# A state-space layer: scan results and their products with C share one ring of four chunks, and GpSimd multiplies in place

## The chip, the cores and the metric

The kernel runs on one core of one Trainium2 chip. A core has five engines that run their own instruction streams and meet at semaphores: TensorE (PE in the profile, its weight loads PEld), VectorE (DVE), ScalarE (ACT), GpSimd (POOL) and SyncE (SP), which here issues DMAs. The metric is the device time of one execution in microseconds (us), lower is better.

## The reference, cut to what matters

The whole program is a tower of nine layers on 8 images of 257 tokens. The change lies in one layer, a bidirectional state-space layer with 512 inner channels and 32 states for each:

```python
def step(h, ins):
    dt_t, B_t, C_t, u_t = ins
    dA = jnp.exp(dt_t[..., None] * A)
    h = dA * h + (dt_t * u_t)[..., None] * B_t[:, None, :]
    y = jnp.einsum('bdn,bn->bd', h, C_t)
    return (h, y)
_, ys = jax.lax.scan(step, h0, xs)          # 257 tokens
y = ys.transpose(1, 0, 2) + uc * Dp
y = y * _silu(z)
```

It runs forward over each image with one set of weights and backward with another.

## The kernel before, in words

The layer is `section_mamba`. It treats 16 units one after the other: 8 images forward, then 8 backward. Channels lie on the 128 partitions in four blocks j. A unit has 16 chunks n: q = n // 4 is a group of 8 states, j = n % 4 a block of channels. A chunk is a tile of 128 x 8 x 256 numbers (8 states, the first 256 tokens), and is cut into four parts m of two states each.

For a part, the engines work as a line:

- ScalarE writes the decays exp(dt * A) into `da` (two chunks deep, line 2326).
- TensorE spreads B over the partitions into PSUM `pb` (four parts deep, `spread_b`, line 2114). In chunks 4 to 15 the last part comes ready multiplied from transposes instead (`turn_products`, line 2101).
- VectorE multiplies `pb` by dt * u (`product`, line 2494; not for the turned parts), then scans the part into `hs` (line 2513).
- GpSimd multiplies half a chunk of `hs` (four states) by C, which lies in `cb`, into `hc` (line 2013), two halves to a chunk. Between them it copies the states of token 255 into `h_l` (line 2012).
- TensorE adds up the eight states of a chunk with matmuls against the identity into PSUM `py` (`total`, line 2127).

`hs` and `hc` hold two chunks each. The order of every engine's stream is written out by hand. TensorE's step (n, m) is: spread part 4n + m + 2, then `total` of part m of chunk n - 2, then other work. So `total` of the first half of a chunk stands ahead of the spreads that VectorE needs two chunks later. VectorE, before it scans part p, makes the product for part p + 1; that stands ahead of the scan in its stream. Before the first scan of chunk n it waits until GpSimd has multiplied all of chunk n - 2 (`hc_done`). GpSimd starts the first half of chunk n when two of its parts are scanned (`b_free`) and when TensorE has added up chunk n - 2 (`y_free`); it starts the second half when all four are scanned.

Between chunks the engines do the rest of the unit and prepare the next one. On GpSimd: after chunk 0 `last_token` (the 257th token of the unit before, by five small instructions, lines 1979 to 1986) and three memsets; in chunk 2 `last_gate` (lines 1992 and 1995); after chunks 3 and 4 `taps` (three adds each, line 1935, the convolution of the next unit); small `cut`s after 8 and 9; after 10 line 1974; after 11 `cut_low` (lines 1949 and 1950); after 12 and 13 `soften` (lines 1958 to 1960). On TensorE: `outward` (line 2138) at the four steps of chunk 5, projections for the next unit (line 2058) at the steps (6,1), (6,2), (7,0) and (7,1), `b_c_rank` at (8,0). On ScalarE: `take_z` follows the projections of chunks 6 and 7 and ends with a Silu and a table load; only then come the decays of chunk 8 and the scaled transposes `tp` (line 2348). VectorE reduces the last token's sum (`out_last`, line 2471) after the first scan of chunk 2; for this it waits for `last_token`.

Of the kernel before, what the change touches and what calls it, by code (L numbers as in the profile page):

```python
# [1781 lines left out]
def section_mamba(nc, k, con, dirs, bfuse, normed=0):  # L1782
# [6 lines left out]
    L = T - 1  # L1789
    open_section(nc, k, "mamba")  # L1790
    with ExitStack() as ctx:
# [21 lines left out]
        hs = sb("hs", [P, 2, NQ_, L])  # L1813
        hc = sb("hc", [P, 2, NQ_, L])
# [11 lines left out]
                 "sqd var std scaled normed f_done f_out conv_link soft_link soft_low soft_top last_link act_head act_tail").split()  # L1826
# [48 lines left out]
        with nc.Block() as block:  # L1875
# [43 lines left out]
            def _(pool):  # L1919
# [77 lines left out]
                def body(u, v, d, before, after):  # L1997
                    scanned, summed = Turn(u, SUB, 4), Turn(u, NCH, 2)
                    for n in range(NCH):
                        q, j = n // DJ, n % DJ  # L2000
                        if j == 0:
                            pool.wait_ge(s["c_odd" if q % 2 else "c_even"], Turn(u, 32)(16 * (q // 2 + 1)))
                        for half in range(2):
                            part_ = slice(4 * half, 4 * half + 4)
                            pool.wait_ge(s["b_free"], scanned(4 * n + 2 * half + 2))
                            if half == 0:
                                pool.wait_ge(s["y_free"], summed(n - 1))
                            settle(pool, k)
                            if (n, half) == (2, 1) and before is not None:
                                last_gate(u - 1, 1 - v)  # L2010
                            if half:
                                nc.gpsimd.tensor_copy(h_l[:, v, j, q * NQ_:(q + 1) * NQ_], hs[:, n % 2, :, L - 1])
                            nc.gpsimd.tensor_tensor(hc[:, n % 2, part_], hs[:, n % 2, part_], cb[:, q % 2, part_, :], ALU.mult).then_inc(s["hc_done"], 1)  # L2013
                        if n == 0 and before is not None:
                            last_token(u - 1, 1 - v, before)
                        if n == 10:
                            last_rate(u, v, d)
                        if after is not None:
                            if n == 0:
                                pool.wait_ge(s["dt_set"], Turn(u, DJ)(DJ))  # L2020
                                settle(pool, k)
                                lead(1 - v)
                            if n in (3, 4):
                                taps(u + 1, 1 - v, n - 3)
                            if n in (8, 9):
                                cut(u + 1, n - 8)
                            if n == 11:
                                cut_low(u + 1, 1 - v, 0, 4, 0)
                            if n == 12:
                                soften(u + 1, 1 - v, 0, 2, 4)  # L2030
                            if n == 13:
                                soften(u + 1, 1 - v, 2, 4, 8)
# [16 lines left out]
            def _(pe):  # L2049
# [67 lines left out]
                def total(u, v, d, n, m):  # L2117
# [7 lines left out]
                    for o in range(2):  # L2125
                        st = 2 * m + o
                        ins = nc.tensor.matmul(sums(j), k.ident[:], hc[:, n % 2, st, :], start=False, stop=(q == QN - 1 and st == NQ_ - 1 and j % 2 == 1))  # L2127
# [311 lines left out]
            def _(dve):  # L2439
# [56 lines left out]
                def body(u, v, d, before, after):  # L2496
                    for n in range(NCH):
                        for m in range(4):
# [6 lines left out]
                            if m == 0:  # L2505
                                dve.wait_ge(s["hc_done"], Turn(u, 2 * NCH, 16)(2 * n - 2))
# [6 lines left out]
                            nc.vector.tensor_tensor_scan(two(hs[:, n % 2, 2 * m:2 * m + 2, :]), two(da[:, n % 2, 2 * m:2 * m + 2, :]), two(pb[:, p % 4]), 0.0, ALU.mult, ALU.add).then_inc(s["b_free"], 1)  # L2513
# [1059 lines left out]
```

## Time and profile before

| what | us |
|---|---|
| median of 3 runs | 3731.81 (3726.15 to 3732.51) |
| the profiled execution | 3738.08 |
| its span | 3736.3 |
| first to last start of the scans of line 2513 | 1168.9 to 2972.6 |
| busy in the whole span | PE 3177.2, DVE 2509.6, ACT 2060.3, POOL 1907.3 |

The page gives, for each engine, busy time; the span in 40 slices; then the groups of instructions with the idle time of the engine in front of them and what ended it. The layer takes some 1,800 of the 3,736 us. In its slices VectorE stands at nine tenths or more, TensorE at eight, GpSimd at eight or nine, ScalarE at seven. A timeline row gives a start, a length, an engine and a line; in square brackets stand the idle time ahead of it and who ended it. "x2" is two instructions without a gap.

### The profile page before, as it was taken

Reading aid. Unit: us, or ns where it says so; the run is one execution under the profiler, and the core shown is the slowest. Engines: PE = TensorE matmul, PEld = TensorE weight load, DVE = VectorE, ACT = ScalarE, POOL = GpSimd, SP = SyncE. Lnnn points to the kernel's source line nnn. Section 1 sums busy time; section 2 is a strip of 40 time slices with the busy share of each in tenths; the row PEclk is TensorE's granted clock in tenths of the full one; section 3 lists DMA queues with packets and bytes.
Section 4 is the critical chain, followed back from the end, with each engine's and each line's share of the span. In section 5 each row is a group of like instructions: output and inputs, shape, how many; then the busy total and the mean of one; then the engine's idle time right before and its main releaser. Section 6 shows DMA issues by size and latency. Waiting matters only on the chain. (4 is left out here: it accounts for less than half of the span.)

```text
span 3736.3 us, 61028 instructions
## 1 busy us (share of the span) xinstructions
PE 3177.2 (85%) x19916; PEld 2391.4 (64%) x19916; DVE 2509.6 (67%) x3780; ACT 2060.3 (55%) x4490; POOL 1907.3 (51%) x1672
## 2 busy tenths in 40 slices
PE   0959989989986889888888888898888887999957
PEld 0649976668974566666666666666665665666544
DVE  6351126653126999999999999999999833666541
ACT  0232225551226778777777778777777433666522
POOL 0013312200315898898888898988898600000024
PEclk9779989999997999999999999999999997999965
DMA  3039930012951111111111111111111000000036
GB/s 104 1 122 332 334 112 2 2 42 104 331 200 64 35 36 46 36 35 47 35 49 46 35 37 35 47 35 35 36 46 35 23 12 15 2 2 2 1 96 200
DMA packets 134796, 262.22 MB, mean 70 GB/s; under 512 B 13792, under 2 KB 106328, under 8 KB 123960
## 3 DMA queue, kind: packets, MB, share of 16 engines
q1 hardware_dynamic: 124568, 230.99, 18.8%
q0 software_dynamic: 9888, 27.01, 2.2%
q8 instruction: 175, 2.87, 0.3%
q14 instruction: 165, 1.35, 0.1%
HBM read 233.42 MB, written 24.55 MB: 69 GB/s over the span
## 5 line engine op out<-in xcount | busy, mean ns | idle before, releaser
L2013 POOL TENSOR_TENSOR ssm_hc<-ssm_hs,ssm_cb 128x1024 f32<-128x1024 f32 x512 | 1205.3, 2358 | 178.0 <-PE ssm_py L2127 157.9
L2513 DVE TENSOR_TENSOR_SCAN ssm_hs<-ssm_da,ssm_pb 128x512 f32<-128x512 f32 x1024 | 1222.0, 1208 | 96.0 <-POOL ssm_hc L2013 91.3
L2127 PE MATMUL ssm_py<-ssm_hc,ident 128*128 128x256 f32 x4096 | 1069.2, 384 | 39.2 <-POOL ssm_hc L2013 39.2
L2326 ACT ACTIVATE ssm_da<-ssm_dt,ssm_an 128x255 f32<-128x255 f32 x2048 | 863.8, 498 | 194.1 <-DVE ssm_hs L2513 155.5
L2127 PEld LDWEIGHTS ssm_py<-ssm_hc,ident 128*128 128x128 f32 x4096 | 709.8, 192 | 119.4 <-POOL ssm_hc L2013 47.2
L2494 DVE TENSOR_TENSOR ssm_pb<-ssm_pb,ssm_dtu 128x512 f32<-128x512 f32 x832 | 563.7, 678 | 49.1 <-PE ssm_pb L2114 25.6
L2114 PE MATMUL ssm_pb<-ssm_bst,ssm_eyeb 96*128 96x256 bf16 x1664 | 327.9, 279 | 140.3 <-DVE ssm_hs L2513 121.8
L2114 PEld LDWEIGHTS ssm_pb<-ssm_bst,ssm_eyeb 96*128 96x128 bf16 x1664 | 133.1, 99 | 346.2 <-DVE ssm_hs L2513 248.7
L3353 DVE TENSOR_TENSOR moe_hid<-moe_pu,moe_actg 128x512 f32<-128x512 f32 x71 | 49.1, 692 | 349.1 <-PE moe_pu L2988 349.1
L2988 PEld LDWEIGHTS moe_pu<-moe_xt,moe_up 128*128 128x128 f32 x2272 | 266.8, 193 | 6.4 <-ACT moe_xt L3113 3.0
L2988 PE MATMUL moe_pu<-moe_xt,moe_up 128*128 128x128 f32 x2272 | 267.8, 277 | 1.8 <-ACT moe_xt L3113 1.8
L2858 POOL DMA_INDIRECT moe_xr<-moe_x_dram,moe_rowx x71 | 69.0, 971 | 334.1 <-PE ln_ps L2975 180.0
L1662 DVE TENSOR_REDUCE duo_mxr<-duo_pairs 128x4 f32<-128x1024 f32 x128 | 156.7, 1224 | 101.8 <-PE duo_pairs L1400 76.7
L1570 ACT ACTIVATE duo_ex<-duo_pairs 128x1024 f32<-128x1024 f32 x128 | 131.0, 1023 | 98.0 <-PE duo_pairs L1400 97.9
L2101 PE MATMUL ssm_pb<-ident,ssm_tp 128*128 128x128 f32 x768 | 119.7, 279 | 47.7 <-ACT ssm_tp L2348 34.4
L1396 PE MATMUL duo_pairs<-duo_k,duo_q 32*128 32x256 f32 x1024 | 151.5, 413 | 9.0 <-DVE duo_mxr L1662 3.7
L1400 PE MATMUL duo_pairs<-duo_q,duo_k 32*128 32x256 f32 x1024 | 145.0, 399 | 1.2 <-ACT duo_ex L1570 1.1
L2101 PEld LDWEIGHTS ssm_pb<-ident,ssm_tp 128*128 128x128 f32 x768 | 92.4, 142 | 80.1 <-DVE ssm_hs L2513 52.4
L2058 PE MATMUL ln_ps<-x,ssm_win 128*128 (+1 forms) x512 | 134.7, 387 | 4.0 <-DVE x L351 1.8
L3003 PE MATMUL ln_ps<-moe_down,moe_hid 128*128 128x256 f32 x568 | 134.5, 380 | 1.1 <-ACT moe_yo L3134 1.1
L2864 POOL DMA_INDIRECT moe_y_dram<-moe_yo,moe_rowy x71 | 70.2, 988 | 118.9 <-ACT moe_yo L3134 118.9
L2348 ACT ACTIVATE ssm_tp<-ssm_dtut,ssm_bt 128x512 f32<-128x512 f32 x192 | 125.2, 708 | 0.0
(591 smaller groups left out, 5195.8 us busy)
## 6 DMA issues: line engine op xcount, KB each, us to landing
moe_up<-in_moe_up SPq DMA_DIRECT2D x72, 1024.0 KB, 6.1
ssm_cb<-ssm_c_dram SPq DMA_DIRECT2D x64, 1024.0 KB, 5.6
moe_down<-in_moe_down SPq DMA_DIRECT2D x72, 512.0 KB, 7.1
sw_wt<-in_sw_w SPq DMA_DIRECT2D x64, 192.5 KB
moe_x_dram<-moe_tok SPq DMA_DIRECT2D x32, 128.0 KB
moe_yg<-moe_y_dram SPq DMA_DIRECT2D x16, 256.0 KB, 3.3
tok_w<-in_wd SPq DMA_DIRECT2D x4, 576.0 KB, 12.8
out<-h SPq DMA_DIRECT2D x1, 2056.0 KB, 6.4
```

Source lines behind the costliest of these rows:

```text
L1396: ins1 = nc.tensor.matmul(dst1[:, o, at], q[r, b1, t * P:t * P + P], kk[r, b1, a, 0:256], start=True, stop=True)
L1400: ins2 = nc.tensor.matmul(dst2[:, o, at], kk[r, b2, a, t * P:t * P + P], q[r, b2, 0:256], start=True, stop=True)
L1662: released(nc.vector.tensor_reduce(mxr[:, u % 2, a, 2 * jp:2 * jp + 2, :], bank("s1", u, a, jp).rearrange("p o (t s) -> p o t s", t=2), AX ...
L2013: nc.gpsimd.tensor_tensor(hc[:, n % 2, part_], hs[:, n % 2, part_], cb[:, q % 2, part_, :], ALU.mult).then_inc(s["hc_done"], 1)
L2058: ins = nc.tensor.matmul(pm[:, n % 2, 0:T], w_in[:, c, n * P:n * P + P], row, start=(c == 0), stop=(c == C - 1))
L2101: ins = nc.tensor.transpose(pb[:, p % 4, o, h * P:h * P + P], tp[:, TURNED.index(q) % 2, o, h, j * P:j * P + P], k.ident[:])
L2114: ins = nc.tensor.matmul(pb[:, p % 4, o, :], one_state(st), bst2[:, v, 0:L], start=True, stop=True)
L2127: ins = nc.tensor.matmul(sums(j), k.ident[:], hc[:, n % 2, st, :], start=False, stop=(q == QN - 1 and st == NQ_ - 1 and j % 2 == 1))
L2326: ins = nc.scalar.activation(da[:, n % 2, 2 * m + o, 1:L], dt2[:, v, j, 1:L], ACT.Exp, scale=a_n[:, d, j, st:st + 1])
L2494: nc.vector.tensor_tensor(b2, b2, dtu2[:, v, j:j + 1, 0:L].broadcast_to([P, 2, L]), ALU.mult).then_inc(s["b_set"], 1)
L2513: nc.vector.tensor_tensor_scan(two(hs[:, n % 2, 2 * m:2 * m + 2, :]), two(da[:, n % 2, 2 * m:2 * m + 2, :]), two(pb[:, p % 4]), 0.0, ALU.m ...
L2988: ins = nc.tensor.matmul(pu[:, b % 2, g, j * P:j * P + P], up[:, b % WR, c, g * HID + j * P:g * HID + j * P + P], xt[:, b % 2, c, :], star ...
```

## The change

`hs` becomes a ring of four chunks and `hc` goes away. GpSimd multiplies each half of a chunk in place in `hs`. Since that destroys the states, the copy of token 255's states now comes before both halves, after all four parts are scanned, and GpSimd waits for its own copy (a new semaphore `h_kept`) before it multiplies. Its wait for `y_free` goes. `last_gate` moves from the middle of chunk 2 to the front of chunk 3. TensorE's `total` reads `hs`. VectorE's wait before chunk n is now for `y_free` of chunk n - 4, in place of `hc_done` of chunk n - 2.

```diff
+    RING = 4
-        hs = sb("hs", [P, 2, NQ_, L])
-        hc = sb("hc", [P, 2, NQ_, L])
+        hs = sb("hs", [P, RING, NQ_, L])
...
                 def body(u, v, d, before, after):
-                    scanned, summed = Turn(u, SUB, 4), Turn(u, NCH, 2)
+                    scanned = Turn(u, SUB, 4)
                     for n in range(NCH):
                         q, j = n // DJ, n % DJ
                         if j == 0:
                             pool.wait_ge(s["c_odd" if q % 2 else "c_even"], Turn(u, 32)(16 * (q // 2 + 1)))
+                        pool.wait_ge(s["b_free"], scanned(4 * n + 4))
+                        if n == 3 and before is not None:
+                            last_gate(u - 1, 1 - v)
+                        settle(pool, k)
+                        nc.gpsimd.tensor_copy(h_l[:, v, j, q * NQ_:(q + 1) * NQ_], hs[:, n % RING, :, L - 1]).then_inc(s["h_kept"], 1)
+                        pool.wait_ge(s["h_kept"], Turn(u, NCH)(n + 1))
                         for half in range(2):
-                            part_ = slice(4 * half, 4 * half + 4)
-                            pool.wait_ge(s["b_free"], scanned(4 * n + 2 * half + 2))
-                            if half == 0:
-                                pool.wait_ge(s["y_free"], summed(n - 1))
-                            settle(pool, k)
-                            if (n, half) == (2, 1) and before is not None:
-                                last_gate(u - 1, 1 - v)
-                            if half:
-                                nc.gpsimd.tensor_copy(h_l[:, v, j, q * NQ_:(q + 1) * NQ_], hs[:, n % 2, :, L - 1])
-                            nc.gpsimd.tensor_tensor(hc[:, n % 2, part_], hs[:, n % 2, part_], cb[:, q % 2, part_, :], ALU.mult).then_inc(s["hc_done"], 1)
+                            part_ = hs[:, n % RING, 4 * half:4 * half + 4, :]
+                            nc.gpsimd.tensor_tensor(part_, part_, cb[:, q % 2, 4 * half:4 * half + 4, :], ALU.mult).then_inc(s["hc_done"], 1)
...
                     for o in range(2):
                         st = 2 * m + o
-                        ins = nc.tensor.matmul(sums(j), k.ident[:], hc[:, n % 2, st, :], start=False, stop=(q == QN - 1 and st == NQ_ - 1 and j % 2 == 1))
+                        ins = nc.tensor.matmul(sums(j), k.ident[:], hs[:, n % RING, st, :], start=False, stop=(q == QN - 1 and st == NQ_ - 1 and j % 2 == 1))
...
-                            if m == 0:
-                                dve.wait_ge(s["hc_done"], Turn(u, 2 * NCH, 16)(2 * n - 2))
+                            if m == 0 and (n >= RING or before is not None):
+                                dve.wait_ge(s["y_free"], Turn(u, NCH, 2)(n - RING + 1))
                             dve.wait_ge(s["da_done"], Turn(u, SUB)(p + 1))
...
-                            nc.vector.tensor_tensor_scan(two(hs[:, n % 2, 2 * m:2 * m + 2, :]), two(da[:, n % 2, 2 * m:2 * m + 2, :]), two(pb[:, p % 4]), 0.0, ALU.mult, ALU.add).then_inc(s["b_free"], 1)
+                            nc.vector.tensor_tensor_scan(two(hs[:, n % RING, 2 * m:2 * m + 2, :]), two(da[:, n % 2, 2 * m:2 * m + 2, :]), two(pb[:, p % 4]), 0.0, ALU.mult, ALU.add).then_inc(s["b_free"], 1)
```

Two lines fewer stand above line 2013, so that later lines move up by two; the multiply is line 2011 and the copy line 2007 afterwards.

On GpSimd, in a unit that has one before it, chunk 1 to the front of chunk 3 stood like this (the rows L2013 are halves of chunks 1, 1, 2, 2 and 3):

```order
337 L2013 TENSOR_TENSOR ssm_hc<-ssm_hs,ssm_cb 128x1024
338 L2005 REGISTER_ALU
339 L2012 COPY ssm_hl<-ssm_hs 128x8
340 L2013 TENSOR_TENSOR ssm_hc<-ssm_hs,ssm_cb 128x1024
341 L2005 REGISTER_ALU
342 L2007 REGISTER_ALU
343 L2013 TENSOR_TENSOR ssm_hc<-ssm_hs,ssm_cb 128x1024
344 L2005 REGISTER_ALU
345 L1992 TENSOR_TENSOR ssm_yl<-ssm_yl 128x4
346 L1993 REGISTER_ALU
347 L1995 TENSOR_TENSOR ssm_zs<-ssm_zs,ssm_yl 128x4
348 L2012 COPY ssm_hl<-ssm_hs 128x8
```

Now the same place holds chunk 2, `last_gate`, and chunk 3 with the `taps` behind it:

```order
327 L2003 REGISTER_ALU
328 L2007 COPY ssm_hl<-ssm_hs 128x8
329 L2008 REGISTER_ALU
330 L2011 TENSOR_TENSOR ssm_hs<-ssm_hs,ssm_cb 128x1024 x2
331 L2003 REGISTER_ALU
332 L1992 TENSOR_TENSOR ssm_yl<-ssm_yl 128x4
333 L1993 REGISTER_ALU
334 L1995 TENSOR_TENSOR ssm_zs<-ssm_zs,ssm_yl 128x4
335 L2007 COPY ssm_hl<-ssm_hs 128x8
336 L2008 REGISTER_ALU
337 L2011 TENSOR_TENSOR ssm_hs<-ssm_hs,ssm_cb 128x1024 x2
338 L1932 ISA
```

The copy has moved from between the halves to ahead of them, and the gate from inside chunk 2 to ahead of chunk 3's copy.

At the head of such a unit, chunk 0 and `last_token` stood like this:

```order
319 L2013 TENSOR_TENSOR ssm_hc<-ssm_hs,ssm_cb 128x1024
320 L2005 REGISTER_ALU
321 L2012 COPY ssm_hl<-ssm_hs 128x8
322 L2013 TENSOR_TENSOR ssm_hc<-ssm_hs,ssm_cb 128x1024
323 L1979 TENSOR_TENSOR ssm_yl<-ssm_uc,ssm_cols 128x4
324 L1981 TENSOR_TENSOR ssm_tl<-ssm_dtu,ssm_bcl 128x128
```

Now:

```order
308 L2007 COPY ssm_hl<-ssm_hs 128x8
309 L2008 ISA
310 L2011 TENSOR_TENSOR ssm_hs<-ssm_hs,ssm_cb 128x1024 x2
311 L1979 TENSOR_TENSOR ssm_yl<-ssm_uc,ssm_cols 128x4
```

Both halves now stand behind the copy, ahead of `last_token`.

## Rows read from the trace of the kernel before

**Rows 1.** Page, groups: count, busy and mean ns, idle before and releaser.
```profile
L2013 POOL TENSOR_TENSOR ssm_hc<-ssm_hs,ssm_cb 128x1024 f32<-128x1024 f32 x512 | 1205.3, 2358 | 178.0 <-PE ssm_py L2127 157.9
L2513 DVE TENSOR_TENSOR_SCAN ssm_hs<-ssm_da,ssm_pb 128x512 f32<-128x512 f32 x1024 | 1222.0, 1208 | 96.0 <-POOL ssm_hc L2013 91.3
```

**Rows 2.** Waits of DVE in the layer, 1169 to 2973: total us, times, longest.
```profile
DVE ssm_hs L2513 <- POOL ssm_hc L2013: 91.3, 46, 2.7
DVE ssm_pb L2494 <- PE ssm_pb L2114: 25.6, 22, 2.6
```

**Rows 3.** Windows of two units: length, busy PE, PEld, DVE, ACT, POOL; PEclk.
```profile
1620.97:1736.01 115.04, 98.56 (x502) 74.34 (x501) 106.06 (x124) 85.54 (x193) 100.71 (x76) 0.99 0.13 39
1736.01:1849.00 112.99, 98.07 (x509) 74.01 (x507) 105.64 (x124) 85.47 (x193) 100.54 (x76) 1.00 0.13 39
```

**Rows 4.** Timeline of DVE, one unit and the next's head.
```profile
2309.00 1.21 DVE L2513 TENSOR_TENSOR_SCAN ssm_hs<-ssm_da,ssm_pb 128x512 f32<-128x512 f32 x1
...
2330.35 1.21 DVE L2513 TENSOR_TENSOR_SCAN ssm_hs<-ssm_da,ssm_pb 128x512 f32<-128x512 f32 x1
...
2352.75 1.22 DVE L2513 TENSOR_TENSOR_SCAN ssm_hs<-ssm_da,ssm_pb 128x512 f32<-128x512 f32 x1 [1.76 <-POOL ssm_hc L2013]
...
2364.34 0.70 DVE L2494 TENSOR_TENSOR ssm_pb<-ssm_pb,ssm_dtu 128x512 f32<-128x512 f32 x1 [1.29 <-PE ssm_pb L2114]
...
2384.26 1.21 DVE L2513 TENSOR_TENSOR_SCAN ssm_hs<-ssm_da,ssm_pb 128x512 f32<-128x512 f32 x1
...
2407.33 1.22 DVE L2513 TENSOR_TENSOR_SCAN ssm_hs<-ssm_da,ssm_pb 128x512 f32<-128x512 f32 x1 [1.89 <-POOL ssm_hc L2013]
...
2416.24 1.22 DVE L2513 TENSOR_TENSOR_SCAN ssm_hs<-ssm_da,ssm_pb 128x512 f32<-128x512 f32 x1 [2.57 <-POOL ssm_hc L2013]
...
2431.71 0.26 DVE L2471 TENSOR_REDUCE ssm_yl<-ssm_tl 128x4 f32<-128x128 f32 x1
```

**Rows 5.** Timeline of POOL, the same unit.
```profile
2310.37 0.19 POOL L2012 COPY ssm_hl<-ssm_hs 128x8 f32<-128x8 f32 x1 [0.24 <-DVE ssm_hs L2513]
...
2314.15 0.46 POOL L1985 TENSOR_TENSOR ssm_tl<-ssm_tl,ssm_hl 128x128 f32<-128x128 f32 x1
2314.68 0.46 POOL L1986 TENSOR_TENSOR ssm_tl<-ssm_tl,ssm_bcl 128x128 f32<-128x128 f32 x1
...
2325.00 0.20 POOL L1992 TENSOR_TENSOR ssm_yl<-ssm_yl 128x4 f32<-128x4 f32 x1 [0.50 <-DVE ssm_hs L2513]
...
2325.52 0.19 POOL L2012 COPY ssm_hl<-ssm_hs 128x8 f32<-128x8 f32 x1
2325.68 2.36 POOL L2013 TENSOR_TENSOR ssm_hc<-ssm_hs,ssm_cb 128x1024 f32<-128x1024 f32 x1
...
2332.10 2.36 POOL L2013 TENSOR_TENSOR ssm_hc<-ssm_hs,ssm_cb 128x1024 f32<-128x1024 f32 x1
...
2347.83 2.35 POOL L2013 TENSOR_TENSOR ssm_hc<-ssm_hs,ssm_cb 128x1024 f32<-128x1024 f32 x1 [0.33 <-POOL ssm_e L1935]
...
2386.22 0.19 POOL L2012 COPY ssm_hl<-ssm_hs 128x8 f32<-128x8 f32 x1
...
2413.53 0.19 POOL L2012 COPY ssm_hl<-ssm_hs 128x8 f32<-128x8 f32 x1
...
2418.28 0.19 POOL L2012 COPY ssm_hl<-ssm_hs 128x8 f32<-128x8 f32 x1
```

**Rows 6.** Timeline of PE, the same unit.
```profile
2351.18 1.03 PE L2127 MATMUL ssm_py<-ssm_hc,ident 128*128 128x256 f32 x4
...
2362.57 0.65 PE L2101 MATMUL ssm_pb<-ident,ssm_tp 128*128 128x128 f32 x4 [2.33 <-ACT ssm_tp L2348]
...
2404.81 1.88 PE L2127 MATMUL ssm_py<-ssm_hc,ident 128*128 128x256 f32 x4 [1.22 <-POOL ssm_hc L2013]
```

**Rows 7.** Timeline of the layer's end, all engines.
```profile
2970.31 3.43 DVE L2513 TENSOR_TENSOR_SCAN ssm_hs<-ssm_da,ssm_pb 128x512 f32<-128x512 f32 x3
...
2974.18 2.36 POOL L2013 TENSOR_TENSOR ssm_hc<-ssm_hs,ssm_cb 128x1024 f32<-128x1024 f32 x1
```

More of the change, by code:

```diff
@@ L1825, in section_mamba @@
                  "dt_free dt_exp dt_set crow_in c_out c_even c_odd dtut_done dtut_in tp_in b_done b_free da_done b_set hc_done y_free ys_done o_done o_out "
-                 "sqd var std scaled normed f_done f_out conv_link soft_link soft_low soft_top last_link act_head act_tail").split()
+                 "sqd var std scaled normed f_done f_out conv_link soft_link soft_low soft_top last_link act_head act_tail h_kept").split()
         s = {n: signal(nc, k.sems, "ssm_" + n) for n in names}
```

## The prediction

> **What bounds the kernel now.** I read the groups of the page first. Only the state-space layer is touched, and its two longest groups are GpSimd's multiply and VectorE's scan, which wait for each other: the scan has 91.3 us of idle time in front of it that GpSimd ended, the multiply 157.9 us that TensorE's sums ended [rows 1]. The waits of VectorE inside the layer come next: 91.3 us in 46 pieces of at most 2.7 us for GpSimd, 25.6 us for TensorE's spreads [rows 2]. Then the windows of whole units: in a unit of 112.99 us VectorE is busy 105.64, GpSimd 100.54 and TensorE 98.07 [rows 3]. So VectorE sets the pace with 7.3 us of idle time in a unit, GpSimd has only 5 us less work, and TensorE 7.6 us less. Taking a buffer's limit away can give at most those idle microseconds, and two engines stand close behind.
>
> Last I walked through one unit, to see where the waits are. There are three for GpSimd: 1.76 us at chunk 7, 1.89 at chunk 15 and 2.57 at chunk 0 of the next unit; and one of 1.29 us for a spread, at the product for chunk 9's first part, right behind the first [rows 4]. They come where GpSimd's other work is thick: the taps after chunks 3 and 4, and `cut_low` and `soften` after 11 to 13.
>
> **The change part by part.** I write S(n) for the start of the fourth scan of chunk n, and count from it.
>
> Removed, VectorE's wait for chunk n - 2. It is not the last link between GpSimd and VectorE: TensorE's stream still holds the `total` of chunk n - 2 ahead of the spreads that VectorE needs for the last part of chunk n and for chunk n + 1, and that `total` still waits for GpSimd. So VectorE's freedom grows by about half a chunk, not by two. The new wait, for the sum of chunk n - 4, lies behind that one always, and I cost it at nothing.
>
> Removed, GpSimd's wait for `y_free` (the 157.9 us). It costs nothing now where GpSimd would have waited for scans anyway, and the next item replaces it by a later release.
>
> Moved, the copy ahead of both halves. GpSimd now starts a chunk when its fourth part is scanned, not the second. The copy that waits for the fourth scan today starts 1.37 us after that scan's start (2309.00 to 2310.37) [rows 4, 5]. So copy(n) is at S(n) + 1.37 at the earliest.
>
> Added, the wait for its own copy. The trace has linked small instructions: 2314.15 to 2314.68 is 0.53 us for a length of 0.46, so 0.07 more than the length; copy to multiply without link is 0.16 us (2325.52 to 2325.68) [rows 5]. 0.19 + 0.07 - 0.16 = 0.10 us in each chunk. Bounds: nothing, if it hides, and 0.2 if the register instruction ahead of the wait counts too. 256 times 0.1 would be 26 us of GpSimd's work, of which only what lies on a path counts, below. The multiply itself, in place, keeps its 2.36 us.
>
> Moved, `last_gate`: 0.52 us (2325.00 to 2325.52) [rows 5], now in front of chunk 3, behind the wait for its fourth scan and ahead of the taps. TensorE needs it only in chunk 5, behind a `total` that waits longer.
>
> *The tight place at the unit's seam.* From S(11), at 2384.26, the reduction of `out_last` starts after 47.45 us (2431.71) [rows 4], 4.46 of it the waits at chunks 15 and 0; VectorE's own work is 43.0. Afterwards GpSimd's path is: copy(11) at 1.37; copy 11 to copy 14 takes 27.31 now [rows 5], with three links 27.6; chunks 14 and 15 take 4.75 each (2413.53 to 2418.28), with links 9.7; from copy(0) to the end of `last_token` 4.77 now (2310.37 to 2314.68 + 0.46), and then 2.36 more, since the copy stands ahead of both halves, and 0.1: 7.2. With 0.1 to reach VectorE the sum is 46.0 us. VectorE is there at 43.0, so it waits 3 us, part of it for the spreads behind `total` of chunk 14, the rest at the reduction, which waits for nothing today. Today's way takes 47.45. Gain 1.5 us a unit. The new late one is `out_last`.
>
> *The tight place at chunks 3 to 8.* TensorE's `total` of chunk 5's first half starts at 2351.18, that is S(3) + 20.83, 1.00 us after that half is multiplied (2347.83 + 2.35) [rows 4 to 6]. Afterwards: copy(3) at 1.37 + 0.52 = 1.89; the second half of chunk 3 at 1.89 + 0.26 + 2.36 = 4.51; from there to chunk 5 is 15.73 us now (2332.10 to 2347.83), 15.83 with the link; copy(5) at 20.34, its first half done at 20.34 + 0.26 + 2.35 = 22.95. So TensorE must wait 2.1 us longer before this `total`. Behind it stand the last two projections, behind them ScalarE's `take_z`, and behind that the decays of chunk 8 and the `tp` for which TensorE waits 2.33 us at 2362.57 [rows 6]. That chain, not GpSimd, is what VectorE meets at chunks 8 and 9: it waits 1.29 us there although it has just lost 1.76 [rows 4]. Without the 1.76 it would wait 3.05; after the change 3.05 + 2.1. Loss 2.1 us a unit. The wait for GpSimd that disappears at chunk 7 pays nothing.
>
> *The end.* The last scans end at 2973.74 and the last multiply at 2976.54, 2.80 later [rows 7]. Afterwards 1.37 - 1.21 for the copy's start, 0.26 to the first half, and 2 x 2.36: 5.1. Loss 2.3 us, once.
>
> Each seam comes 15 times and so do the taps. Sum: 15 x 2.1 - 15 x 1.5 + 2.3 = 11.3 us. Against the profiled execution's own 3738.08 that gives 3749.4; it stood 6.3 above the median of the runs, so against the median 3731.8 it gives 3743.
>
> **The rivals.**
>
> *A. TensorE's chain stretches.* If the `total` of chunk 5 is not what holds the projections, or ScalarE makes up for it, only the seam counts: 3731.8 - 22.5 + 2.3 = 3712. For it: TensorE is busy for 98 of a unit's 113 us [rows 3], so it has some air. Against it: between chunk 5 and chunk 8 the timeline shows it without a gap.
>
> *B. The ring does all it can:* every wait for GpSimd goes and none comes: 3731.8 - 91.3 + 2.3 = 3643. Against it: the spread wait behind chunk 7, and GpSimd's path at the seam, which is work and not waiting.
>
> *C. The two places cancel.* 0.5 us off either estimate moves the sum by 7.5 us; 3732.
>
> *D. TensorE's clock.* TensorE waits longer in two places of each unit. Where it has waited 1.22 us for GpSimd, four matmuls take 1.88 us in place of 1.03 [rows 6], the lower of its two levels; a unit in which such a fall meets the spreads takes 115.04 us in place of 112.99 [rows 3]. I count three such units in the trace. If the longer waits make it so in the other twelve: 12 x 2.05 = 24.6 more, 3768. It decides from the point where the longer gaps at chunks 7 and 0 bring a fall in most units.
>
> The Trainium skill, in "TensorE: Matmul & The Clock Gate", Part 1, says that the clock is gated by how busy the engine has been, half rate when idle; by that rule longer waits speak for this rival, and the trace agrees in its one case above but shows no general rate.
>
> **How the numbers follow.** My sum has 0.42, A 0.20, B 0.06, C 0.17, D 0.15. What a measurement here can tell from no change is about 0.2%, 7.5 us. Faster by more: A and B, 0.26. Slower by more: D and nearly all of my case, 0.53. Within: C and the rest, 0.21. The likeliest case's own range is 3735 to 3755 (0.5 us in each place, 0.1 in each link). Leaving out B and the far end of D, 3708 to 3770.
>
> **What would show it.** Right: the waits of the scan for GpSimd nearly gone from the waits of VectorE, but idle time for spreads and decays at chunks 8 and 9 of 4 to 5 us a unit; the reduction of line 2469 waiting for GpSimd, 0.5 to 3 us in 15 units; TensorE waiting some 2 us for GpSimd ahead of the `total` in chunk 7; units of 113.5 to 114 us. Wrong: no such wait of TensorE there and units under 112.5 (A), under 108 (B); units of 115 and more with PEclk below 0.97 (D); a multiply that isn't 2.36 us in place.

## The result, and the profile after

| | before | after |
|---|---|---|
| median of 6 runs, side by side | 3732.16 us (3720.88 to 3732.90) | 3751.77 us (3741.60 to 3766.17) |
| the profiled execution | 3738.08 us | 3746.07 us |

The ratio is 1.0063, with a 95% interval of 1.0036 to 1.0090: the changed kernel is slower, by 19.6 us between the medians. The forecast was 11.3 us more, 3743.

The groups of the page that answer to [rows 1]:

```profile
L2511 DVE TENSOR_TENSOR_SCAN ssm_hs<-ssm_da,ssm_pb 128x512 f32<-128x512 f32 x1024 | 1219.6, 1205 | 20.7 <-ACT ssm_da L2324 17.7
L2125 PE MATMUL ssm_py<-ssm_hs,ident 128*128 128x256 f32 x4096 | 1105.5, 394 | 119.6 <-POOL ssm_hs L2011 119.4
L2011 POOL TENSOR_TENSOR ssm_hs<-ssm_hs,ssm_cb 128x1024 f32<-128x1024 f32 x512 | 1195.1, 2355 | 20.9 <-POOL ssm_hl L2007 0.4
L2492 DVE TENSOR_TENSOR ssm_pb<-ssm_pb,ssm_dtu 128x512 f32<-128x512 f32 x832 | 564.3, 678 | 152.0 <-PE ssm_pb L2112 123.3
L2007 POOL COPY ssm_hl<-ssm_hs 128x8 f32<-128x8 f32 x256 | 49.2, 192 | 169.1 <-DVE ssm_hs L2511 147.2
```

The scan no longer waits for GpSimd, and GpSimd no longer waits for TensorE's sums. Both waits came back in other names. The sums wait 119.4 us for the products, GpSimd's copy 147.2 us for the scans, and VectorE's product 123.3 us for the spreads. The multiply in place takes what it took before, 2355 ns.

The waits inside the layer (total us, times, longest), which answer to [rows 2]:

```profile
DVE ssm_pb L2492 <- PE ssm_pb L2112: 123.3, 76, 4.4
PE ssm_py L2125 <- POOL ssm_hs L2011: 117.7, 59, 3.4
DVE ssm_hs L2511 <- ACT ssm_da L2324: 13.3, 12, 1.1
DVE ssm_yl L2469 <- POOL ssm_tl L1986: 2.4, 6, 0.5
```

VectorE's waits for GpSimd and for spreads were 91.3 + 25.6 = 116.9 us. Now the waits for spreads, decays and the last token are 139.0. So the change swapped one wait for a slightly larger one.

The windows of 14 units, from one reduction of the last token to the 14th after it, before and then after (columns as in [rows 3]):

```profile
1297.09:2885.33 1588.24, 1380.05 (x7050) 1043.05 (x7049) 1479.51 (x1737) 1195.56 (x2701) 1408.67 (x1048) 0.99 0.13 39
```

```profile
1294.53:2913.16 1618.63, 1412.46 (x7053) 1084.26 (x7052) 1483.39 (x1736) 1191.19 (x2703) 1415.28 (x1051) 0.96 0.13 39
```

A unit takes 113.45 us before and 115.62 after, so 2.17 us more; the forecast was 0.6. VectorE's and GpSimd's work is all but the same. PEclk fell from 0.99 to 0.96, and TensorE's busy time rose by 32 us.

To find where the 2.17 us lie, I took the starts of the fourth scans, S(n), in 13 whole units of each trace and averaged the stretches:

| stretch | before | after | forecast |
|---|---|---|---|
| S(3) to S(9) | 41.03 | 44.39 | +2.1 |
| S(9) to S(11) | 13.08 | 13.09 | 0 |
| S(11) to S(2) of the next unit | 52.55 | 51.44 | -1.5 |
| S(2) to S(3) | 6.84 | 6.83 | 0 |

All of the loss is in the first row, and it has levels. In five of the 14 units after, S(3) to S(9) took 43.0 us, in three 43.5 to 44.2, and in six 45.2 to 45.7. Before, the undisturbed units took 40.8.

VectorE in an undisturbed unit of the kernel after, where S(3) is 2350.02 and S(9) is 2392.99:

```profile
2350.02 1.21 DVE L2511 TENSOR_TENSOR_SCAN ssm_hs<-ssm_da,ssm_pb 128x512 f32<-128x512 f32 x1
...
2377.30 0.70 DVE L2492 TENSOR_TENSOR ssm_pb<-ssm_pb,ssm_dtu 128x512 f32<-128x512 f32 x1 [2.70 <-PE ssm_pb L2112]
...
2380.81 1.22 DVE L2511 TENSOR_TENSOR_SCAN ssm_hs<-ssm_da,ssm_pb 128x512 f32<-128x512 f32 x1 [1.11 <-ACT ssm_da L2324]
...
2386.14 0.70 DVE L2492 TENSOR_TENSOR ssm_pb<-ssm_pb,ssm_dtu 128x512 f32<-128x512 f32 x1 [1.29 <-PE ssm_pb L2112]
...
2392.99 1.21 DVE L2511 TENSOR_TENSOR_SCAN ssm_hs<-ssm_da,ssm_pb 128x512 f32<-128x512 f32 x1
```

GpSimd in the same unit, up to the first half of chunk 5:

```profile
2351.43 0.20 POOL L1992 TENSOR_TENSOR ssm_yl<-ssm_yl 128x4 f32<-128x4 f32 x1 [1.93 <-DVE ssm_hs L2511]
...
2351.95 0.19 POOL L2007 COPY ssm_hl<-ssm_hs 128x8 f32<-128x8 f32 x1
2352.22 2.36 POOL L2011 TENSOR_TENSOR ssm_hs<-ssm_hs,ssm_cb 128x1024 f32<-128x1024 f32 x1
...
2370.48 4.65 POOL L2011 TENSOR_TENSOR ssm_hs<-ssm_hs,ssm_cb 128x1024 f32<-128x1024 f32 x2
```

TensorE in the same unit, at the `total` of chunk 5 and the projections behind it:

```profile
2372.87 1.13 PE L2125 MATMUL ssm_py<-ssm_hs,ident 128*128 128x256 f32 x4 [1.86 <-POOL ssm_hs L2011]
2373.84 1.03 PE L2056 MATMUL ln_ps<-x,ssm_win 128*128 x4
2374.70 0.60 PE L2099 MATMUL ssm_pb<-ident,ssm_tp 128*128 128x128 f32 x4
2375.14 1.03 PE L2125 MATMUL ssm_py<-ssm_hs,ident 128*128 128x256 f32 x4
2376.01 1.03 PE L2056 MATMUL ln_ps<-x,ssm_win 128*128 x4
2376.87 0.39 PE L2112 MATMUL ssm_pb<-ssm_bst,ssm_eyeb 96*128 96x256 bf16 x2
```

This `total` starts at S(3) + 22.85, two us later than in [rows 6], and the spread for which VectorE waits 2.70 us is the last row. Behind the second projection stands ScalarE's `take_z`, then the decays of chunk 8 (line 2324) and the transposes `tp` (line 2346), for which TensorE waits:

```profile
2377.07 0.38 ACT L2255 ACTIVATE ssm_zs<-ln_ps 128x257 f32<-128x257 f32 x1 [1.78 <-PE ln_ps L2056]
...
2379.72 3.29 ACT L2324 ACTIVATE ssm_da<-ssm_dt,ssm_an 128x255 f32<-128x255 f32 x8
2382.92 1.32 ACT L2346 ACTIVATE ssm_tp<-ssm_dtut,ssm_bt 128x512 f32<-128x512 f32 x2
2384.37 0.65 PE L2099 MATMUL ssm_pb<-ident,ssm_tp 128*128 128x128 f32 x4 [2.33 <-ACT ssm_tp L2346]
```

VectorE's second and third wait, 1.11 and 1.29 us, are for these decays and for the spread behind these transposes. Its three waits sum to 5.1 us.

The same place in a disturbed unit (S(3) = 1885.21), first TensorE, then VectorE:

```profile
1908.07 1.98 PE L2125 MATMUL ssm_py<-ssm_hs,ident 128*128 128x256 f32 x4 [1.87 <-POOL ssm_hs L2011]
1909.84 1.91 PE L2056 MATMUL ln_ps<-x,ssm_win 128*128 x4
```

```profile
1914.17 0.70 DVE L2492 TENSOR_TENSOR ssm_pb<-ssm_pb,ssm_dtu 128x512 f32<-128x512 f32 x1 [4.39 <-PE ssm_pb L2112]
```

The wait for GpSimd is the same, 1.87 us, but behind it TensorE runs at the lower of its two levels: 1.98 and 1.91 us in place of 1.13 and 1.03. VectorE's wait grows from 2.70 to 4.39. The windows S(3) + 21 to S(3) + 38 of these two units, the disturbed one first:

```profile
1906.21:1923.21 17.00, 12.81 (x54) 9.83 (x55) 10.02 (x11) 9.61 (x20) 13.76 (x8) 0.86 0.01 1
2371.02:2388.02 17.00, 12.82 (x68) 10.20 (x69) 11.90 (x14) 11.30 (x24) 13.72 (x8) 1.00 0.01 1
```

In that window PEclk was 1.00 in the five units of 43.0 us and below it in the other nine; before it was below 1.00 in 3 of 14.

At the seam behind the undisturbed unit, VectorE (at "issue" the trace names no releaser):

```profile
2432.13 1.21 DVE L2511 TENSOR_TENSOR_SCAN ssm_hs<-ssm_da,ssm_pb 128x512 f32<-128x512 f32 x1
2434.69 0.70 DVE L2492 TENSOR_TENSOR ssm_pb<-ssm_pb,ssm_dtu 128x512 f32<-128x512 f32 x1 [1.35 <-issue]
...
2440.32 0.70 DVE L2492 TENSOR_TENSOR ssm_pb<-ssm_pb,ssm_dtu 128x512 f32<-128x512 f32 x1 [1.79 <-PE ssm_pb L2112]
...
2443.30 0.70 DVE L2492 TENSOR_TENSOR ssm_pb<-ssm_pb,ssm_dtu 128x512 f32<-128x512 f32 x1 [0.86 <-PE ssm_pb L2112]
...
2453.58 0.26 DVE L2469 TENSOR_REDUCE ssm_yl<-ssm_tl 128x4 f32<-128x128 f32 x1
```

S(11) is 2406.06 here, so the reduction of this seam, one of the longest, comes after 47.52 us and waits for nothing. GpSimd's last token was ready 1.1 us before it:

```profile
2452.02 0.46 POOL L1986 TENSOR_TENSOR ssm_tl<-ssm_tl,ssm_bcl 128x128 f32<-128x128 f32 x1
```

Over 14 units GpSimd ended the last token 46.08 us after S(11), and the reduction came after 46.54 us on average (before: 47.67).

The end of the layer answers to [rows 7]:

```profile
2999.29 2.30 DVE L2511 TENSOR_TENSOR_SCAN ssm_hs<-ssm_da,ssm_pb 128x512 f32<-128x512 f32 x2
3001.76 0.19 POOL L2007 COPY ssm_hl<-ssm_hs 128x8 f32<-128x8 f32 x1 [0.71 <-DVE ssm_hs L2511]
3002.04 4.65 POOL L2011 TENSOR_TENSOR ssm_hs<-ssm_hs,ssm_cb 128x1024 f32<-128x1024 f32 x2
```

From the end of the scans to that of the multiplies it is 5.1 us, as forecast (2.80 before).

In this one pair of traces the 14 units are 30.4 us longer and the layer, from its first scan to its last, 32.9; the executions differ by only 8.0. The other 25 us lie outside the layer: up to its first scan the trace after is 5.1 us shorter (1163.8 in place of 1168.9), behind its last scan 19.9 (742.7 in place of 762.6). The 762.6 is the odd one: in the 11 other traces of this document that part takes 741 to 749 us. The interval of the ratio is 13 to 34 us and holds what the layer lost.

### The profile page after: what moved, and what is told of

Its sections match the earlier page's. It is cut to its first block and busy times, and to the rows that moved or that the text cites. A ratio compares the mean times of both kernels' runs of the same rounds, so it can differ in the third digit from the quotient of the medians.

```text
span 3744.3 us, 60553 instructions
## 1 busy us (share of the span) xinstructions
PE 3198.8 (85%) x19916; PEld 2426.2 (65%) x19916; DVE 2512.2 (67%) x3780; ACT 2054.2 (55%) x4490; POOL 1913.3 (51%) x1672
## 5 line engine op out<-in xcount | busy, mean ns | idle before, releaser
L2125 PE MATMUL ssm_py<-ssm_hs,ident 128*128 128x256 f32 x4096 | 1105.5, 394 | 119.6 <-POOL ssm_hs L2011 119.4
L2011 POOL TENSOR_TENSOR ssm_hs<-ssm_hs,ssm_cb 128x1024 f32<-128x1024 f32 x512 | 1195.1, 2355 | 20.9 <-POOL ssm_hl L2007 0.4
L2125 PEld LDWEIGHTS ssm_py<-ssm_hs,ident 128*128 128x128 f32 x4096 | 729.7, 197 | 215.4 <-POOL ssm_hs L2011 137.9
L2492 DVE TENSOR_TENSOR ssm_pb<-ssm_pb,ssm_dtu 128x512 f32<-128x512 f32 x832 | 564.3, 678 | 152.0 <-PE ssm_pb L2112 123.3
L2112 PEld LDWEIGHTS ssm_pb<-ssm_bst,ssm_eyeb 96*128 96x128 bf16 x1664 | 146.5, 100 | 237.5 <-DVE ssm_hs L2511 129.3
L2007 POOL COPY ssm_hl<-ssm_hs 128x8 f32<-128x8 f32 x256 | 49.2, 192 | 169.1 <-DVE ssm_hs L2511 147.2
```

Of the source, the lines that this page charges most:

```text
L2011: nc.gpsimd.tensor_tensor(part_, part_, cb[:, q % 2, 4 * half:4 * half + 4, :], ALU.mult).then_inc(s["hc_done"], 1)
L2112: ins = nc.tensor.matmul(pb[:, p % 4, o, :], one_state(st), bst2[:, v, 0:L], start=True, stop=True)
L2125: ins = nc.tensor.matmul(sums(j), k.ident[:], hs[:, n % RING, st, :], start=False, stop=(q == QN - 1 and st == NQ_ - 1 and j % 2 == 1))
L2492: nc.vector.tensor_tensor(b2, b2, dtu2[:, v, j:j + 1, 0:L].broadcast_to([P, 2, L]), ALU.mult).then_inc(s["b_set"], 1)
```

## The experiments

Each ran in five rounds beside the kernel before. The chips of the three groups gave 3720.25, 3708.95 and 3722.23 us for the kernel before, so the ratios count. The table has the stretches of the trace as above (13 units), the unit and PEclk over 14 units. These are of one traced execution each, the ratio is of all; the traced execution stood within 9 us of its kernel's median, but for "early in 3, 4, 5" (15 us under it), "filled at chunk 7" (15 above) and "later sums" (19 above). In the last three kernels VectorE's output products or its reduction stand in later chunks, so that 0.7 to 0.9 us of a unit have moved from the second stretch into the one from S(2) to S(3).

| kernel | S(3) to S(9) | S(11) to S(2) | unit | PEclk | ratio to before |
|---|---|---|---|---|---|
| before | 41.03 | 52.55 | 113.45 | 0.99 | 1 |
| after | 44.39 | 51.44 | 115.62 | 0.96 | 1.0063 [1.0036, 1.0090] |
| late start alone | 42.39 | 54.02 | 116.31 | 0.97 | 1.0132 [1.0093, 1.0170] |
| early start everywhere | 42.12 | 50.41 | 112.47 | 0.96 | 0.9959 [0.9931, 0.9986] |
| early in 3, 4, 5 | 41.61 | 51.34 | 112.86 | 0.97 | 1.0017 [0.9996, 1.0038] |
| early in 12 to 15, 0 | 44.64 | 52.51 | 117.02 | 0.95 | 1.0155 [1.0133, 1.0176] |
| early in 3 and 11 | 42.13 | 50.06 | 112.16 | 0.96 | 0.9922 [0.9891, 0.9953] |
| filled at the seam | 44.09 | 51.83 | 115.86 | 0.99 | 1.0090 [1.0061, 1.0120] |
| filled at chunk 7 | 43.46 | 51.36 | 114.78 | 0.96 | 1.0041 [1.0016, 1.0066] |
| later sums | 41.83 | 50.28 | 112.75 | 0.97 | 0.9951 [0.9926, 0.9976] |
| later sums, reduction later | 41.61 | 47.28 | 109.59 | 0.99 | 0.9877 [0.9851, 0.9903] |
| the same, early start everywhere | 41.37 | 47.26 | 109.36 | 0.99 | 0.9861 [0.9837, 0.9886] |

**The late start alone**, in the kernel before:

```diff
-                            pool.wait_ge(s["b_free"], scanned(4 * n + 2 * half + 2))
                             if half == 0:
+                                pool.wait_ge(s["b_free"], scanned(4 * n + 4))
                                 pool.wait_ge(s["y_free"], summed(n - 1))
...
-                            if half:
+                            if half == 0:
                                 nc.gpsimd.tensor_copy(
```

> The kernel before with one edit: GpSimd copies ahead of both halves and so starts a chunk after its fourth scan; scan results and products stay in separate buffers of two chunks, without the wait of GpSimd for its own copy. Theory L (the late start is what costs, the ring gives nothing because TensorE's order holds VectorE anyway): as slow as the changed kernel, 3744 to 3760, TensorE's waits for the products near 118 us in the layer, as after. Rival M (the ring gave something back, and the late start costs more than the difference shows): clearly slower than the changed kernel, 3765 or more, with VectorE's scans waiting over 91 us for GpSimd. Rival N (the cost lies in the multiply in place or in the link to the copy): not slower than before, 3725 to 3738.

Rival M holds: 1.0132, and the scans' wait for GpSimd grows from 91.3 to 148.5 us:

```profile
DVE ssm_hs L2513 <- POOL ssm_hc L2013: 148.5, 75, 2.7
PE ssm_py L2127 <- POOL ssm_hc L2013: 75.6, 56, 2.1
```

So the ring was not worth nothing. It gives back 2.6 us at the seam (54.02 to 51.44). Between chunks 3 and 9 it gives nothing back. There the late start alone costs 1.36 us a unit. By the forecast's own terms it should cost 2.1 less the gate (0.52) and three links (0.3), 1.3. The kernel after differs from this one in the links, the gate and GpSimd's missing wait for `y_free` too; no run tests these one by one.

**The early start given back everywhere**, with the ring kept:

```diff
-                        pool.wait_ge(s["b_free"], scanned(4 * n + 4))
                         if n == 3 and before is not None:
                             last_gate(u - 1, 1 - v)
-                        settle(pool, k)
-                        nc.gpsimd.tensor_copy(h_l[:, v, j, q * NQ_:(q + 1) * NQ_], hs[:, n % RING, :, L - 1]).then_inc(s["h_kept"], 1)
-                        pool.wait_ge(s["h_kept"], Turn(u, NCH)(n + 1))
                         for half in range(2):
+                            pool.wait_ge(s["b_free"], scanned(4 * n + 2 * half + 2))
+                            settle(pool, k)
+                            kept = slice(q * NQ_ + 4 * half, q * NQ_ + 4 * half + 4)
+                            nc.gpsimd.tensor_copy(h_l[:, v, j, kept], hs[:, n % RING, 4 * half:4 * half + 4, L - 1]).then_inc(s["h_kept"], 1)
+                            pool.wait_ge(s["h_kept"], Turn(u, 2 * NCH)(2 * n + half + 1))
```

> The changed kernel with the early start given back: GpSimd waits for two scans, copies four states, waits for that copy and multiplies that half in place; then the same for the other half; the gate of the last token stands ahead of chunk 3's waits. The ring of four stays. Theory L (late start): 3720 to 3738, TensorE's waits for the products fall from 118 us to under 60, units near 113. Its price is one more copy with its link in each chunk, 0.3 us of GpSimd. Rival N (in place or the links cost): stays at 3745 or more. Rival R (the ring gives something once the start is early): under 3720.

0.9959 in place of 1.0063, and faster than before. The late start is the cause: this kernel still multiplies in place and has twice as many copies with links, so these are not what made the other slower. The gate has come forward with the start, and no run moves it alone. Times the 3732 us before, 0.9959 is 3717, so that rival R holds beside theory L: with the early start the ring gives something. TensorE's wait for the products fell only to 69.5 us, not below 60. The group of the small copies shows their price, 46.8 us more of GpSimd's time than the 49.2 us of the whole copies:

```profile
L2009 POOL COPY ssm_hl<-ssm_hs 128x4 f32<-128x4 f32 x512 | 96.0, 188 | 80.1 <-DVE ssm_hs L2512 68.5
```

**Where the late start costs.** The same edit for some chunks alone, `if n in EARLY`. First chunks 3, 4 and 5:

> The changed kernel with the early start (four states copied after two scans, then multiplied, then the other half) in chunks 3, 4 and 5 alone, and the gate of the last token ahead of chunk 3's waits. Theory P (the loss lies where the prediction put it, in the chain from chunk 3 over the sum of chunk 5 and the projections to the decays of chunk 8, 2.1 us a unit): units of 113.2 to 114.0 us in place of 115.6, ratio to the kernel before 0.994 to 1.001. Rival S (it lies at the unit's seam, chunks 12 to 0): units stay at 115 or more, ratio 1.004 or more.

Theory P: S(3) to S(9) falls from 44.39 to 41.61, the seam stays, and the unit is 112.86, a little below the expected 113.2. The ratio, 1.0017, is a little above its 1.001, but its interval reaches to 0.9996 and, on the other side, just touches that of the changed kernel, so that what was gained rests on the trace. Then chunks 12 to 15 and 0:

> The changed kernel with the early start in chunks 12 to 15 and 0 alone. Theory P (the seam is no loss against the kernel before, since it takes 47.5 us from the fourth scan of chunk 11 in both): units of 114.6 to 115.6, what is gained comes only from a seam that gets shorter than before; ratio 1.001 to 1.007. Rival S (the late start costs at the seam): units of 113.9 or less, ratio under 1.000.

Neither: it is slower, 117.02. The last token now ends 47.46 us after S(11) in place of 46.08. Those 1.4 us are the five more copies at 0.28 us from copy to multiply (2351.95 to 2352.22 above). The reduction now waits for it in 12 units:

```profile
DVE ssm_yl L2475 <- POOL ssm_tl L1986: 11.2, 12, 1.3
```

Behind the start of chunk 11 GpSimd has no idle time worth the name at the seam, so starting its chunks earlier gives nothing and each added copy is paid in full. Ahead of chunk 11 it stands idle, in the changed kernel:

```profile
2407.44 0.19 POOL L2007 COPY ssm_hl<-ssm_hs 128x8 f32<-128x8 f32 x1 [1.52 <-DVE ssm_hs L2511]
```

That suggested the next one, chunks 3 and 11 alone, where its unbroken stretches begin:

> The changed kernel with the early start in two chunks alone, 3 and 11, and the gate ahead of chunk 3's waits. Theory H (GpSimd has work without a pause from chunk 3, with the taps, and from chunk 11, with the cut and the softening; only where such a stretch begins does the late start cost, behind it GpSimd is late anyway): the stretch S(3) to S(9) falls from 44.4 us to 41.0 to 42.2, S(11) to S(2) of the next unit from 51.4 to 49.0 to 50.2, units 110.5 to 112.3, ratio 0.980 to 0.993. Rival (every chunk's late start costs its part, as in the kernel with the early start in 12 to 15 and 0, which lost): S(11) to S(2) stays at 51 or more, units 113 or more.

Theory H: all four numbers in their ranges, if near their slow ends. The early start of chunk 11 takes 1.4 us off the seam, where five early chunks inside it added 1.1. GpSimd ends the last token 44.74 us after S(11) in place of 46.08, so 1.3 us earlier, for the 1.52 for which it had stood idle.

**TensorE's clock.** Matmuls of no use in TensorE's waits; first at the seam:

```diff
+                            if after is not None and (n, m) in ((14, 2), (15, 0), (15, 2)):
+                                for _ in range(6):
+                                    nc.tensor.matmul(pm[:, 1, 0:L], k.ident[:], uc2[:, v, 0, 0:L], start=True, stop=True)
```

> The changed kernel with six matmuls of no use (into the free half of the bank of sums for projections) ahead of TensorE's waits in the steps (14,2), (15,0) and (15,2): 18 more in a unit, 4.6 us of TensorE's time by the four in 1.03 us, which lie in waits of 3.4 and 2.5 us for GpSimd. Theory K (the half clock behind those waits is what makes the seam longer than forecast): fewer stretches of half clock, VectorE's waits for spreads at the seam (0.35, 1.35, 1.79 and 0.86 us in the unit that I walked) fall by half, time 5 to 25 us less than the changed kernel. Rival (the waits for GpSimd alone set the seam, or the added matmuls are late themselves): the same or up to 20 us slower.

The window S(11) + 18 to S(11) + 42 of one unit, of the changed kernel:

```profile
2424.06:2448.06 24.00, 16.68 (x77) 12.78 (x76) 19.66 (x24) 9.18 (x22) 22.83 (x17) 0.86 0.09 17
```

and of the filled one:

```profile
2422.64:2446.64 24.00, 22.88 (x123) 18.87 (x122) 20.71 (x26) 11.14 (x27) 23.23 (x17) 1.00 0.09 21
```

The falls at the seam are gone in all 14 units (PEclk 1.00; it was 0.86 to 0.93 in all 14), and the seam is no shorter: 51.83 us. The rival holds, but in both of its halves, and so the run doesn't tell what the clock costs here. The 18 matmuls are 36 records and take 8.3 us of TensorE's time, not the 4.6 expected, and the second six are late. GpSimd has multiplied the first half of chunk 13 at 2427.37, and TensorE starts its sum 1.7 us later:

```profile
2425.01 2.36 POOL L2011 TENSOR_TENSOR ssm_hs<-ssm_hs,ssm_cb 128x1024 f32<-128x1024 f32 x1
...
2426.45 2.75 PE L2162 MATMUL ln_ps<-ssm_uc,ident 128*128 128x256 f32 x12
2429.05 1.03 PE L2125 MATMUL ssm_py<-ssm_hs,ident 128*128 128x256 f32 x4
```

It is so in 12 of the 13 whole units; in the changed kernel this sum starts 0.05 us after the product. What the changed kernel itself shows is a bound: GpSimd, busy for 22.8 of the window's 24 us, ends the last token 46.08 us after S(11), and the reduction starts at 46.54. So a clock that stays up can give the seam at most 0.5 us, as long as GpSimd's path stays. Then at chunk 7:

```diff
+                            if (n, m) == (7, 0):
+                                pe.wait_ge(s["b_free"], Turn(u, SUB, 4)(28))
+                                for _ in range(14):
+                                    nc.tensor.matmul(pb[:, 3, 0, :], one_state(0), bst2[:, v, 0:L], start=True, stop=True)
```

> The changed kernel with 14 matmuls of no use (into a part of the spreads' bank that is free there) behind the spread of step (7,0), in the 1.86 us in which TensorE waits for the products of chunk 5; at the spreads' 0.22 us for two they take 1.5 us. In the changed kernel the stretch from the fourth scan of chunk 3 to that of chunk 9 took 43.0 us in the units where the clock stayed up and 45.2 to 45.7 in six where it fell behind that wait. Theory K (the half clock is the rest of the loss, 1.3 us a unit on average): 43.0 to 43.4 in nearly all units, units of 114.2 to 115.0 in place of 115.6, time 10 to 25 us less than the changed kernel, ratio 1.000 to 1.004. Rival (the falls come elsewhere instead, or the added matmuls are late): stretches stay mixed or all above 43.5, ratio 1.005 or more.

No unit took 45 us from S(3) to S(9) any more: 42.8 to 44.3 in 14 units. The unit fell by 0.84, the ratio from 1.0063 to 1.0041 (the intervals overlap, so this rests on the trace). The clock was not cured: it still fell in 8 of 14 units, to 0.90 to 0.93, and only 6 stretches stayed within 43.0 us, so that they are as mixed as the rival had them. Of theory K's 1.3 us about two thirds came.

**TensorE's order.** `total` one chunk later, in the changed kernel:

```diff
-                            if n >= 2:
-                                total(u, v, d, n - 2, m)
+                            if n >= 3:
+                                total(u, v, d, n - 3, m)
                             elif before is not None:
-                                total(u - 1, 1 - v, before, NCH - 2 + n, m)
+                                total(u - 1, 1 - v, before, NCH - 3 + n, m)
...
-                                if n in (0, 2) and m in (1, 2):
-                                    out_chunk(u - 1, 1 - v, before, n + m - 1)
+                                if n in (1, 3) and m in (1, 2):
+                                    out_chunk(u - 1, 1 - v, before, n + m - 2)
```

> The changed kernel with TensorE adding up chunk n - 3 in step n in place of chunk n - 2, and VectorE's four output products of the unit before one chunk later to match. Theory T (TensorE's order, not the buffers, is what makes VectorE meet GpSimd's late products; the spreads stand behind the sums): with a chunk more room the waits of TensorE for the products nearly go (118 to under 30 us), VectorE's waits for spreads fall from 123 us to under 50, units of 109 to 111.5 us in place of 115.6, time 3670 to 3710. Rival G (GpSimd's own path at the seam and at the taps is the limit, whatever TensorE's order): the waits move to the sums of the ring or to the last token's reduction, units above 113.5, time 3735 or more.

Both have a part. TensorE's wait for the products is gone from its group, and the waits for spreads fell to 37.7 us:

```profile
L2125 PE MATMUL ssm_py<-ssm_hs,ident 128*128 128x256 f32 x4096 | 1080.8, 387 | 0.0
L2492 DVE TENSOR_TENSOR ssm_pb<-ssm_pb,ssm_dtu 128x512 f32<-128x512 f32 x832 | 564.0, 678 | 64.0 <-PE ssm_pb L2112 37.7
```

But the unit is 112.75, between the 109 to 111.5 of theory T and the 113.5 of rival G, since GpSimd's path ends in the reduction of the last token:

```profile
DVE ssm_yl L2469 <- POOL ssm_tl L1986: 41.7, 15, 3.5
```

The reduction came 46.07 us after S(11), in 12 of 14 units 46.01 to 46.07. So it is moved behind the fourth scan of chunk 2, `(n, m) == (2, 3)` for `(2, 0)`:

> The changed kernel with TensorE adding up chunk n - 3 in step n, and with VectorE's reduction of the last token behind the fourth scan of chunk 2 in place of the first. With the later sums alone VectorE waited 41.7 us in 15 units, 2.8 us each, for the last token of GpSimd at that reduction. Theory W (that wait is what was late there): it goes, units of 109.8 to 111.3 us in place of 112.75, time 25 to 45 us less than with the later sums alone, ratio 0.983 to 0.989. Rival: the next wait, for spreads or decays at chunks 8 and 9, takes its place, units of 112 or more.

The wait is gone and next to nothing took its place: 109.59 us a unit, a little below the 109.8 expected, and 0.9877. VectorE now waits for the ring, that is for the sums of chunk n - 4, but only 4.9 us in 19 pieces. Last, the early start in every chunk on top:

> The same, and with the early start in every chunk (256 copies of four states more, 46 us of GpSimd's busy time with split alone). If GpSimd's late start still matters once TensorE has a chunk of room: units 0.5 to 1.5 us below those without the early start. Rival (GpSimd's work has become the pace, 104 us of a unit with its gaps): no better than without, or up to 1 us a unit worse. I expect the rival.

The unit is 0.23 us shorter, below the half us that would have spoken for the early start, and the intervals overlap: no difference that can be told. Either version beats both kernels, by 1.2% and 1.4% against the kernel before.

## Why the prediction was right, and where its sizes were off

*By its own signs.* The scans' waits for GpSimd are gone, and TensorE waits 1.86 us ahead of the `total` in chunk 7: both were named as signs that the likeliest case is right. But units of 115 and more with PEclk below 0.97 were named as the sign of rival D, and the 14 units have 115.62 us and 0.96. So the likeliest case came with most of rival D on top. That 3751.8 us still lies near the forecast's 3743 is in part luck: in the traces the layer lost 32.9 us, three times the 11.3 of the sum, while the medians differ by 19.6.

*The ring's freedom.* Right between chunks 3 and 9, where it gave nothing. At the seam it was worth 2.6 us, as the late start alone shows. The new wait for `y_free` costs nothing in the changed kernel: no such wait stands among the rows. That GpSimd's removed wait for `y_free` paid nothing was assumed, and no run tests it alone.

*The link.* From copy to multiply 0.27 us in place of 0.16: right. The multiply in place kept its 2.36.

*Chunks 3 to 8.* Right in mechanism and size. GpSimd was forecast to have chunk 5's first half done at S(3) + 22.95; it was 22.8 (2370.48 + 2.35 - 2350.02). VectorE's waits were forecast at 3.05 + 2.1 = 5.15; they are 5.10 in the undisturbed unit. 43.0 less 40.8 is 2.2 us a unit. Giving chunks 3 to 5 their early start and the gate its early place back took 1.5 of these 2.2 us away (41.3 to 41.6 in all but one unit), and nearly all of what the falls of the clock cost.

*The seam.* Mechanism right, gain mis-sized: 1.1 us in place of 1.5. GpSimd's path was forecast at 46.0 us and measured 46.08. But the late one was named wrongly. In most units it was the spreads behind `total` of chunk 14, not `out_last`, which waited 2.4 us in 6 units where I expected 0.5 to 3 us in 15. `out_last` is the limit only once TensorE's order is changed.

*TensorE's clock (rival D)* is the term that was mis-sized most. I kept it apart as a rival with all or nothing in 12 units. It came in addition to the sum. After the 1.86 us wait for chunk 5's products the clock fell in 9 of 14 units, for 1.39 us a unit on average above the undisturbed 43.0; before it was 41.03 less 40.8, 0.23. That is 1.16 us a unit. By that the sum of a unit is 2.2 - 1.1 + 1.16 = 2.26; the stretches give 2.25. The remark that such a fall decides "at chunks 7 and 0" was half wrong: around chunk 0 PEclk is below 1 in every unit, and GpSimd's path leaves it at most 0.5 us to cost.

The Trainium skill, in "TensorE: Matmul & The Clock Gate", Part 1, calls the throttled clock the default state which activity releases. The trace agrees that it falls behind waits: the lower level behind 1.87 us in one unit, and the full one behind 1.86 us in another with the same instructions. No run here shows what tells these two apart.

*The end.* 2.3 us forecast, 5.1 less 2.8 measured.

*Rivals.* A is refuted: the chain through chunk 5's `total` did hold the projections. B is refuted by the same rows. C would need the two places to cancel; they differ by 1.1 us and the clock.

What stays open: why the clock falls in nine units and not in the other five, what a fall costs at the seam within that half us, and why the profiled execution before took some 20 us more than all others behind the layer.

## What to carry to other kernels

A deeper ring frees an engine only as far as the in-order stream that releases it lets it. Look at what stands ahead of the releasing instruction before adding buffers; here the ring came with a late start of GpSimd and lost 0.6%; it paid 0.8% once that start was early again in two chunks, and 1.2% once the sums' place in TensorE's stream and one reduction were moved to use it. A later start of an engine costs where its unbroken stretch of work begins, up to the time for which the engine then stands idle (1.3 of 1.5 us here); inside such a stretch it costs nothing, and added small instructions cost all they take. When a change makes TensorE wait longer, add the price of its lower clock to the sum at each place where VectorE waits behind it, in proportion to the units in which it may fall.

## What the runs showed of the hardware that I had not expected

- Matmuls of no use kept TensorE's granted clock up and gained nothing. With 18 more a unit the seam's PEclk went from 0.86 to 0.93 up to 1.00 and its length from 51.44 to 51.83 us; six of them held the sum behind them up by 1.7 us.
- The clock fell or stayed behind waits of the same length: over the 17 us around them PEclk was 0.86 with one of 1.87 us and 1.00 with one of 1.86 us, and the fall made VectorE's wait behind it 4.39 us in place of 2.70.
- A wait for one's own 0.19 us copy on GpSimd puts 0.27 us between the copy's start and the next instruction's, where 0.16 stood without it; five more such copies lengthened a path by 1.4 us.
- GpSimd's multiply of 128x1024 f32 takes 2355 ns in place and 2358 ns into another buffer.
